# Attention inside a two-sided expert layer: the value products issued two key blocks at a time

## The reference, cut to what matters

```
x = x + 0.5 * ffn(layernorm(x))          # 64 experts, 8 chosen per token, 64 slots each, plus a shared expert
x = x + attention(layernorm(x))
x = x + 0.5 * ffn(layernorm(x))
```

```
Q = x @ wq + bq ; K = x @ wk + bk ; V = x @ wv + bv
Q, K, V reshaped to (B*H, S, D), H = 16 heads of D = 8, S = 512
scores = Q K^T / sqrt(8) ; attn = softmax(scores)
out = (attn @ V reshaped) @ wo + bo + x ; then a layernorm with gamma and beta
```

## Time and profile before

| what | value |
|---|---|
| median of 3 runs | 885.6 us |
| the profiled execution | 886.09 us, span 884.3 us |
| TensorE busy | 676.9 us, 77% of the span |
| VectorE busy | 609.2 us, 69% |
| ScalarE busy | 461.1 us, 52% |
| GpSimd busy | 400.7 us, 45% |
| granted TensorE clock, mean | 0.839 of 2.4 GHz |
| attention core | from about 237 to 659 us of the span |

### The profile page before, as it was taken

How to read it: one execution, slowest core, us unless ns; L and a number is a source line. 1 busy time by engine, 2 the same in 40 slices (tenths; PEclk the granted TensorE clock), 3 DMA queues, 4 the chain that set the end, 5 groups by cost and what they waited for, 6 DMA issues and landing times.

```text
span 884.3 us, 17025 instructions
## 1 busy us (share of the span) xinstructions
PE 676.9 (77%) x5060; PEld 313.2 (35%) x5121; DVE 609.2 (69%) x1562; ACT 461.1 (52%) x1060; POOL 400.7 (45%) x519
## 2 busy tenths in 40 slices
PE   4885665804799999999999999999970388567670
PEld 3643444502233333333333333333210264344440
DVE  4898544364878888888888888888713569854430
ACT  5752222201377777777777777777763675222220
POOL 5584778675432232232232232230005658477872
PEclk9996677555799999999999999999995559666765
DMA  6996443343434544544544544444110130544334
GB/s 186 258 230 189 80 69 63 42 107 73 71 68 90 98 84 92 96 80 93 96 80 93 94 81 94 93 80 96 26 47 6 41 85 19 168 74 71 66 41 110
DMA packets 233724, 80.26 MB, mean 91 GB/s; under 512 B 166888, under 2 KB 226440, under 8 KB 233608
## 3 DMA queue, kind: packets, MB, share of 16 engines
q1 hardware_dynamic: 212936, 64.94, 33.3%
q0 software_dynamic: 12288, 10.49, 7.9%
q10 hardware_dynamic: 8448, 4.20, 1.6%
HBM read 49.94 MB, written 31.49 MB: 92 GB/s over the span
## 4 chain that ended last, share of the span: by engine, by line
PE 46%; POOL 16%; issue 14%; DVE 11%; ACT 7%; DMA 4%; POOLq 0%; ACTq 0%; SPq 0%; DVEq 0%
PE psum L1459 14%; PE psum L1450 12%; PE psum L1437 10%; POOL sums L630 7%; ACT arena L1209 5%; POOL arena L605 4%; DMA sums<-sums_sb,sidx 2%; DVE arena L817 2%; PE psum L1255 1%; DVE arena L813 1%; PE psum L1413 1%; DMA arena<-dispatch_rows,arena 1%; ACT xn_sb L1086 1%; PE psum L1399 1%; PE psum L1332 1%
## 5 line engine op out<-in xcount | busy, mean ns | idle before, releaser
L990 DVE TENSOR_REDUCE arena<-psum 128x2 f32<-128x1024 f32 x256 | 308.6, 1220 | 53.0 <-PE psum L1437 50.0
L1209 ACT ACTIVATE arena<-psum 128x512 f32<-128x512 f32 x512 | 282.1, 600 | 115.6 <-PE psum L1450 105.5
L1437 PE MATMUL psum<-arena 126*128 126x512 bf16 x512 | 197.8, 393 | 9.3 <-DVE arena L990 5.1
L1450 PE MATMUL psum<-arena 128*128 128x512 bf16 x451 | 173.1, 387 | 7.1 <-ACT arena L1209 3.3
L1459 PE MATMUL psum<-arena 128*32 128x512 f32 x1024 | 136.2, 604 | 1.3 <-ACT arena L1200 1.3
L686 POOL CAST arena<-arena 128x256 bf16<-128x256 f32 x32 | 12.7, 396 | 264.5 <-issue 260.5
L630 POOL DMA_INDIRECT sums<-sums_sb,sidx x64 | 102.7, 1604 | 44.7 <-issue 20.6
L1450 PEld LDWEIGHTS psum<-arena 128*128 128x128 bf16 x512 | 50.6, 100 | 150.0 <-ACT arena L1209 122.4
L605 POOL DMA_INDIRECT arena<-dispatch_rows,arena x64 | 64.2, 1004 | 30.1 <-issue 18.3
L1322 PE MATMUL psum<-ident,arena 128*128 128x128 f32 x64 | 23.5, 382 | 53.4 <-DMA arena<-dispatch_rows,arena 53.0
L1437 PEld LDWEIGHTS psum<-arena 126*128 126x128 bf16 x512 | 49.5, 99 | 37.7 <-DVE arena L990 15.0
(11 more groups left out here) (139 smaller groups left out, 1132.5 us busy)
## 6 DMA issues: line engine op xcount, KB each, us to landing
arena<-qk_parts SPq DMA_DIRECT2D x128, 96.0 KB
ctx<-arena SPq DMA_DIRECT2D x32, 256.0 KB, 2.0
qk_parts<-arena SPq DMA_DIRECT2D x32, 192.0 KB, 3.8
dispatch_rows<-xn_sb ACTq DMA_DIRECT2D x16, 256.0 KB, 2.3
arena<-lists SPq DMA_DIRECT2D x16, 256.0 KB, 3.3
sums<-x_sb SPq DMA_DIRECT2D x16, 256.0 KB
arena<-qk_parts SPq DMA_DIRECT2D x64, 64.0 KB
arena<-ctx SPq DMA_DIRECT2D x64, 64.0 KB, 2.4
```

What stands on the lines that cost most here:

```text
L990: dve.tensor_reduce(mx_r[r % 2][:, 2 * p:2 * p + 2], src, X, ALU.max).then_inc(a_mx, 1)
L1209: act.activation(p_r[tau % NPB], bank[4 + tau % 2][:, :], ACT.Exp, scale=SCALE).then_inc(a_P, 1)
L1437: ins = pe.matmul(bank[tau % 4][:, :], heads(q_st[r], rows, g)[:, qt * P:(qt + 1) * P], heads(k_st[r], rows, g), start=True, stop=True)
L1450: pe.matmul(bank[4 + tau % 2][:, :], keys, heads(q_st[r], rows, g), start=True, stop=True)\
```

## The change

Four things are changed.

1. A table `P_SET = (0, 1, 0, 1)` names the half of the eight exponential buffers that a key block uses, and the exponential's wait is written as a table `(-1, 0, 1, 2)[kt]`.
2. The value products are issued in groups of two: those of key blocks 2 and 3 of unit n - 1 after substep 1 of step n, those of key blocks 0 and 1 of unit n after substep 9.
3. The value projection `v(n + 3)` is issued behind the second group instead of ahead of substep 10.
4. In the expert stage, round 0's `sum_copy` stands ahead of `match(2)` instead of behind it.

```
+    P_SET = (0, 1, 0, 1)
...
                 for q in range(NQ):
                     if q and q + 1 < NQ:
                         hidden(q + 1)
+                    if q == 0:
+                        sum_copy(0)
                     if q + 2 < NQ:
                         match(q + 2)
-                    sum_copy(q)
+                    if q:
+                        sum_copy(q)
                     if q + 2 < NQ:
                         pick(q + 2)
...
                         if g == 0:
-                            wait(act, a_PV, 4 * n + (kt - 1))
-                        act.activation(p_r[tau % NPB], bank[4 + tau % 2][:, :], ACT.Exp, scale=SCALE).then_inc(a_P, 1)
+                            wait(act, a_PV, 4 * n + (-1, 0, 1, 2)[kt])
+                        act.activation(p_r[4 * P_SET[kt] + g], bank[4 + tau % 2][:, :], ACT.Exp, scale=SCALE).then_inc(a_P, 1)
...
-                        ins = pe.matmul(bank[6][32 * g:32 * g + 32, :], v_r[r][:, g, kt, :], p_r[(4 * kt + g) % NPB],
+                        ins = pe.matmul(bank[6][32 * g:32 * g + 32, :], v_r[r][:, g, kt, :], p_r[4 * P_SET[kt] + g],
...
-                        if tau == 10 and (mid or n + 3 < end):
-                            v(n + 3, at(3))
                         if tau == 14 and (mid or n >= 2):
                             proj(n - 2, at(-2))
                         scores_t(n, r, tau)
                         if mid or n + 2 < end:
                             scores(n + 2, at(2), tau)
-                        if tau == 3 and (mid or n >= 1):
+                        if tau == 1 and (mid or n >= 1):
+                            pv(n - 1, at(-1), 2)
                             pv(n - 1, at(-1), 3)
-                        if tau % 4 == 3 and tau > 3:
-                            pv(n, r, tau // 4 - 1)
+                        if tau == 9:
+                            pv(n, r, 0)
+                            pv(n, r, 1)
+                            if mid or n + 3 < end:
+                                v(n + 3, at(3))
...
+                pv(NT - 1, (NT - 1) % NBUF, 2)
                 pv(NT - 1, (NT - 1) % NBUF, 3)
```

## The result

The changed kernel takes 896.4 us (median of 4 runs, 895.6 to 899.5) against 885.65 us (four runs of the kernel before): a ratio of 1.0123, 95% interval 1.0089 to 1.0156. It is slower, by 1.2%. The forecast was slower, 899 us in a range of 882 to 909.

What follows compares the result with a forecast made beforehand. The prediction took TensorE as the bound in the attention core. To 886.09 us it added 16.8 for attention and took off 3.8 for the earlier copy: 899.1, given as 899 us, in a range of 882 to 909.

Steps and rivals of the forecast that it cites:

- The buffers' table costs nothing: Attention exponentials: same eight buffers, same order and same waits, so cost and gain nothing.
- no DMA moves: Moved value projection in attention: no DMA is issued by any moved step; no time was set for this.
- Seams saved, 0.54 a step: TensorE in an attention step: ten seams (0.90 us) become four (0.36), saving 0.54 us.
- Waits 1, 2 and 3: TensorE waits added per attention step: up to substep 9 0.60 us, at substeps 12 and 13 0.25, before `xT` 0.53.
- ScalarE's idle time of about 2 us: Sign expected in the attention trace: ScalarE idle about 2 us twice a step, ahead of the exponentials of substeps 0 and 8.
- rival A: Attention: TensorE stays the bound, ScalarE and VectorE catch up, only savings remain; 865 us, chance 0.10.
- The sum of a step: Full attention step: added waits less saved seams and the old 0.28 us hole, +0.56 us, over 25 steps 14.0 us.
- The seven other steps: Attention steps other than the 25 full ones, where links are missing: 0 to 0.7 us each, 2.8 together.
- Attention +16.8: Whole attention core: full steps and the other seven together make it 16.8 us slower, +-6 us.
- The copy, -3.8: Both expert stages: round 0's earlier copy lets the first scatter go 1.90 and 1.89 us earlier, saving 3.8 us.
- Rival B: Attention: added waits come to just 0.82 us a step, only the copy's gain is left; 882 us, chance 0.08.
- Rival C: Attention: TensorE's clock falls to 1.2 GHz in one step in ten, costing 40 us; 939 us, chance 0.08.

Runs made afterwards that it cites:

- e5: The changed kernel with the output projection issued before substep 12 instead of 14 and `z_add` behind `row_max` p = 5 instead of 6: 887.7 us, ratio 0.9998.
- e8: The changed kernel with `row_max` over only the first 256 of each 512 keys, part of the computation left out: 880.3 us, ratio 0.9911.
- e9: The kernel before with only the first group of value products (after substep 1) and the late copy of the sums: 893.9 us, ratio 1.0072.
- e11: The kernel before with `row_max` over only the first 256 of each 512 keys, part of the computation left out: 885.4 us, ratio 0.9978.
- e3: The changed kernel with twelve exponential buffers instead of eight, some small tiles moved in SBUF: 894.6 us, ratio 1.0089.
- e1: The changed kernel with round 0's copy of the sums put back behind `match(2)`, leaving only the attention part: 898.7 us, ratio 1.0136.
- e2: The kernel before with only round 0's copy of the sums moved ahead of `match(2)`: 882.7 us, ratio 0.9943.
- e6: The changed kernel with `ctx_copy` behind the exponential of substep 7 instead of 5: 894.4 us, ratio 1.0070.

## Why the prediction was right

*The buffers' table costs nothing* and *no DMA moves*: nothing in the runs speaks against it.

*Seams saved, 0.54 a step.* Right, and a little more was there. In a group the passes start 0.453 apart once and then 0.43, so that the four passes with their seams cost 1.95 instead of my 4 x 0.453 + 0.18 = 1.99; two groups give 0.08 that I had not counted. The bound of a seam between two blocks of one kind is settled at 0.

*Waits 1, 2 and 3.* Forecast 0.60, 0.25 and 0.53; measured 0.53, 0.23 and 0.52. Forecast distance from the group's start to the first exponential 1.10, measured 1.13. The wait that ends last before `xT` is VectorE's: it goes when `z_add` comes early (e5) and when VectorE has less to do (e8), it comes back with the first group alone (e9), and the kernel before does not have it (e11). Of the signs, ScalarE's idle time of about 2 us was 2.23 ahead of substep 0 and 1.22 ahead of substep 8. For waits 1 and 2 the walk was right, but one of the reasons beside it was not: in part 1 and in rival A I let the eight buffers hold ScalarE back. e3 takes that wait away and the step does not move. The distances fit the other reason, the tiles that stand behind the group and the two PSUM banks, which no run has tested by itself.

*The sum of a step* was +0.56 and came out at +0.36; by the terms it is 1.28 - 0.28 - 0.54 - 0.08 = 0.38. So the term that was mis-sized is the full step, by 0.10 of waits and 0.08 of faster passes; 0.02 is left over. *The seven other steps*, 2.8 us, came out near 1: 25 full steps of 0.36 are 9.0, and the whole core grew by 10.0.

*Attention +16.8*: measured +10.0 in the profiles, 12 us by the ratio of e1. *The copy, -3.8*: by e2 -5 (-3.2 to -6.9). In the changed kernel's own profile little of it is seen, 0.4 in each stage, because that run's first copy waited for TensorE at a slower moment and because these stages differ by more than a microsecond from run to run.

*How near the total came* is in part luck. The attention core was forecast 6.8 us too high in the profiles. Outside it the forecast took 3.8 us off, and the profiled run shows nothing off there: 0.4 less before the first gather, 0.4 less in each expert stretch, and 1.1 more between the last exponential and the first gather behind it. The two misses point opposite ways.

*Rival A* (865 us) fell: both engines had time to spare on average and could not use it, as it said itself, with waits of 1.28 against the 0.82 from which it would have decided. *Rival B* needed waits of 0.82 to 1.0. *Rival C* (the clock falls): granted 1.00 in the steady attention stretch, before and after, although TensorE now stands at four places of a step for 0.19 to 0.52 us. The Trainium skill ("TensorE: Matmul & The Clock Gate", A second HAM failure mode: psum-queue depth-cycling) says that frequent short idle times between groups of matmuls on cycling banks can make the clock swing; the trace of the changed kernel does not show it with these holes. The Trainium skill ("TensorEngine Tiling (Array Packing)", Key Properties) says that a change of tiling mode drains TensorE and a change of tile does not. The rows agree: about 0.09 on each side of a block of narrow matmuls, none inside a group.

## What to carry to other kernels

Putting like matmuls together saves their seams, but the work that is moved had been covering something where it stood: ask of each old place which chain ran under it (here `row_max`, `z_add`, the shared bank), and what the engines behind it still have to read while the group runs at the new place. An engine's longest idle time need not cost anything; take it away by itself before it is blamed. A half of a change can be a gain and the other half a loss: they should be timed apart.

## What the runs showed of the hardware

- A block of four f32 matmuls, 32 columns each and 512 wide, costs 0.09 us at its entry next to 128-column matmuls (489.48 to 489.57). Inside a run of such blocks the passes start 0.453 apart at first and 0.43 later, with no seam at the block's edge. From the last pass's start to the next matmul it is 0.54 in both kernels (490.03 to 490.57 before), that is 0.09 at the exit if the last pass counts 0.453, or 0.11 if it counts 0.43.
- From a 512-wide bf16 matmul's start to the start of the exponential that reads it, 0.43 us; from the exponential's start to the matmul that may reuse the bank, 0.65. With two banks a pair of substeps should thus take 1.08 us at least (an estimate from these two; substeps 10 to 12 of the e8 trace take 480.19 to 481.27 = 1.08), where TensorE's own work in it is 4 x 0.22 = 0.88.
- In e6, from the end of a copy out of PSUM to the value products that wait for it: 0.24 us in the loop, where a register operation of TensorE's queue lies between, and 0.10 in the steps outside it.
